# Extra storage for the keys and queries of the first attention, fp32 turns of the rounded activations, and a new written order of all engines

## The chip, the cores and the metric

The kernel runs on one core of a Trainium2 chip. The metric is the device time of one execution in microseconds (us). The kernel before took 265.31, 265.40 and 266.64 us in three runs, median 265.4. Of one more execution a profile was recorded; that one took 264.35 us. The engines are TensorE (PE, with weight loads shown apart as PEld), VectorE (DVE), ScalarE (ACT), GpSimd (POOL) and SyncE (SP, which only issues DMAs).

## The reference, cut to what matters

Two batches (B = 2) of 512 tokens with 128 features pass four blocks, each added to the running x after a scale by a tanh gate:

```python
x = x + tanh(g_xattn[0]) * L0_xattn(ctx, layernorm(x))      # 8 heads of 64, 512 queries, 512+77 keys
x = x + tanh(g_ffn[0])   * L0_ffn(layernorm(x))             # 8-bit rounding, 128->512, conv, silu, 512->128
x = x + tanh(g_xattn[1]) * L1_xattn(layernorm(x), ctx, ctx) # 16 heads of 8, 77 keys, rotary positions
x = x + tanh(g_ffn[1])   * L1_ffn(layernorm(x))             # 8 experts, top 2, and a shared one

# first attention, per batch and head
q = ln @ Wq; k, v = split(concat(layernorm(x), ln) @ Wkv)
attn = softmax((q / scale) @ k.T - max); out = (attn @ v) @ Wout

# rounding of the activations in the first feed-forward block
scale = 127.0 / clip(max(abs(h), -1), 1e-5)
hq = clip(round(h * scale), -128, 127) / scale              # h has 512 features per token
y = hq @ round_to_ternary(w2).T
```

## The kernel before, in words

The work is cut into items, each with a kind: x0 (turned, normalised input), q and k (queries and keys of one pair of heads; 4 pairs per batch), v (values), u (scores of one head for 128 queries; 64 of them), w (probabilities times values for one pair and 256 queries; 16), o (output projection), n (layer norm and rounding behind it), f1 to f4 (the feed-forward block: turn, product with w1 and convolution, rounding, product with w2), a1, a2, a3, a4, a6 (second attention: turn, queries, keys, scores, output), m1 to m4 (experts: turn, product up, router, product down). An item has stages: F and B are its first and second work on PE, A1 and A2 on ACT, D0 to D3 on DVE, P1 and P2 on POOL, Ca or Cd a copy out of PSUM by ACT or by DVE.

The order is written out by hand in one long string, PLAN. A word such as `f2:D1` puts the next item of that kind and stage at the end of that engine's list. `u:F6` also names the PSUM bank (0 to 7), and `a4:B+20@2` puts 20 turns of the identity matrix into bank 2 ahead of the stage; they compute nothing that is used. Each engine walks its list strictly in order, and semaphores carry the data dependencies. So an instruction that waits holds up everything behind it on its engine.

Three places are touched.

* Queries and keys. Pair g (0 to 7 over both batches) has its keys, split into an upper part KH and a rest KL, and its queries Q in one of two buffers, g mod 2. ACT writes the upper part (L863, L871), DVE the rest (L1033, L1040), and SP copies half of the keys across partitions. ACT waits before it writes until the last scores of pair g-2 are done.
* Rounding (f3, f4). ACT writes the rounded values plus a constant MAGIC as fp32 (L893). An own copy (L812 on ACT or L814 on DVE, four of each) takes MAGIC off and writes bf16 to QB. PE turns QB four 128x128 pieces at a time (L649) with a bf16 identity made by DVE. ACT copies the bf16 turns to QBT (L898), and PE multiplies by w2 (L731).
* Order. PLAN holds 85 identity turns in all (L518, `slot<-K`), most of them in the part behind the first attention.

The copies of turned probabilities of the second attention are L787 on ACT and L789 on DVE; its maximum is L1152 on DVE. The router is L1163 to L1230 on DVE.

Of the kernel before, what the change touches and what calls it, by code (L numbers as in the profile page):

```python
# [15 lines left out]
P = 128  # L16
# [109 lines left out]
a4:D1 f1:D1 f2:F6 a4:B a2:D1 f2:F7 a1:P1 a4:A1 f2:A1 a4:D1 a4:B a4:Ca f2:A1 a4:Ca f2:F3 f2:D1 f2:A1 f2:F6+4@2 f2:A2 f2:D1 f2:D2 f2:A1 a4:A1 a4:F0
f2:D1 a4:B+20@2 f2:A2 f2:A2 a4:D1 a4:F2 f2:D1 f2:D2 a4:D1 a4:A1 f2:D2 f2:A2 a4:B+11@7 a4:Ca a4:A1 f2:D2 f3:F6 f3:F7 f3:D1 a4:Ca f3:D1 f3:A1 f3:F4 a4:B
a4:F0 f3:Cd f3:F6 a4:D1 a4:Ca f4:F5 f3:A1 a6:F7 f4:A1 f3:D1 f3:D1 a4:A1 f3:Cd f4:B f3:A1 f3:A1 f4:F4 a4:F2 f4:A1 f3:Cd f4:D2 f3:Ca f4:F5 f4:B
f4:A1 f4:F6+2@6 f4:B a4:D1 f4:A1 f4:B+2@4 a4:A1 f4:D2 a4:B f4:P2 f4:D2 f4:D3 f4:D2 a4:F4 a4:Ca a1:F6 a4:D1 a4:B a1:A1 f4:P2 a4:A1 a2:F0 a4:Ca f4:D3
a1:P1 a1:F6+2@1 a2:D1 a4:B+9@1 a6:D1 a4:F2 a4:D1 a1:A1 a4:Ca a4:F0 a4:F4 a6:B a4:D1 a4:A1 a6:D2 a2:F6 a6:P2 a6:F7 a4:A1 a4:D1 a4:B a2:D1 a4:Ca a6:D3  # L130
a6:D1 a4:F2+8@6 a4:D1 a4:B a4:Cd a4:A1 a6:B a4:B a6:D2 m1:F6 a4:A1 a4:Ca a4:F0 a4:B a4:D1 a4:F4 a4:Cd a4:D1 a6:P2 a6:D3 m1:A1 a4:F6 a4:A1 m3:F2
a6:F3 m3:D1 a4:A1 a4:D1 m3:A1 a4:A1 a4:B a4:B a4:B a4:Ca m2:F0 a4:Ca m3:D2 m2:A1 a4:Ca a6:D1 a4:F4 m1:F2 m1:A1 a6:B m2:B a4:D1 m3:F2 m2:F6
a4:A1 m2:P1 m2:A2 a6:D2 a4:B m2:A1 m2:B a4:Ca m2:P1 a1:P1 m3:D1 m2:D1 m2:D2 m2:A2 m3:A1 m2:D1 a6:F3 m4:F0 m3:D2 m4:A1 m2:F4 m2:A1 a6:P2 a6:D1
m2:D2 m2:B m2:A2 m4:B a6:D3 m1:F6 a6:B m4:D2 m2:P1 m2:D1 m2:D2 m4:F0 m1:A1 m3:F2 m2:F6 a6:D2 a6:P2 m2:A1 m2:F4 m4:A1 m3:D1 m2:B m3:A1 m2:P1
m2:A2 m4:B m2:A1 m2:B+2@3 m3:D2 m4:D2 m2:P1 a6:D3 m4:F0 m2:D1 m2:A2 m2:D2 m2:D1 m2:F2 m4:A1 m2:D2 m2:B m2:A1 m1:F6 m2:A2 m1:A1 m4:B m2:P1 m2:D1
m4:F4 m4:A1 m4:D2 m3:F0 m2:F6 m2:D2 m4:B m4:F2 m2:A1 m3:D1 m3:A1 m3:D2 m4:D2 m2:B m4:A1 m2:F0 m2:A2 m4:F4 m2:B m2:A1 m4:B m2:P1 m2:D1 m4:A1
m2:A2 m2:D2 m4:F6 m2:P1 m2:D1 m2:D2 m4:D2 m4:B m4:A1 m4:F0 m4:A1 m4:B m4:B m4:D2 m4:D2 m4:D2
# [49 lines left out]
def mega_kernel(nc, x, ctx, ctxT, cols, wq, wk, wv, wout, w1T, w2T, l1w, bo, wgu, wdT, const, out):  # L187
    stack = ExitStack()
    with stack:
# [26 lines left out]
        identb = sb("identb", [P, P], BF16)  # L216
# [35 lines left out]
        KL = sb("KL", [P, 4, KEVEN], F32R)  # L252
        V = sb("V", [P, 5, IN0])
# [14 lines left out]
        QB = sb("QB", [P, 2, HID], BF16)  # L268
# [10 lines left out]
        PT1 = sb("PT1", [P, 2, 2 * KC1, N])  # L279
# [3 lines left out]
        HM = sb("HM", [P, QT, MT])  # L283
# [36 lines left out]
        identb_ready = sem("identb_ready")  # L320
# [16 lines left out]
        qb_copied = {"ACT": sem("qb_by_act"), "DVE": sem("qb_by_dve")}  # L337
# [466 lines left out]
        def copy_quantised(engine, by, item):  # L804
# [3 lines left out]
            if n > 2:  # L808
                engine.wait_ge(qbt_ready, n - 2)
# [549 lines left out]
```

## Time and profile before

| | |
|---|---|
| median of three runs | 265.4 us |
| profiled execution | 264.35 us |
| its span, first to last instruction | 262.4 us |
| PE busy | 254.0 us (97%) |
| DVE busy | 217.1 us (83%) |
| ACT busy | 192.2 us (73%) |
| POOL busy | 31.1 us (12%) |
| granted TensorE clock | full in all slices |

The span is shorter than the execution by 1.95 us, which lies around the program. Busy time of PE counts the identity turns as well, and a matmul's recorded length is longer than the distance to the next one: identity turns have a mean length of 0.276 us, and 18 of them in a row take 1.97 us from the first start to the next instruction's, 0.109 us each. So what PE really does is read from the distance between starts.

### The profile page before, as it was taken

The numbers are of one execution on the slowest core, as the hardware profiler recorded it, in microseconds if no ns is written. First come the engines' busy times: TensorE is split into PE (matmuls) and PEld (weight loads), VectorE is DVE, ScalarE is ACT, GpSimd is POOL, SyncE is SP. The second block draws the span as 40 slices with busy tenths as digits, with TensorE's granted clock in tenths as the row PEclk, the third lists the DMA queues.
The fourth block names the chain that finished last, engine by engine and source line by source line (L and its number), as shares of the span: only waits on it lengthen the run. The fifth ranks groups of instructions, "written<-read, shape, count | busy, mean of one in ns | idle before, by whom it ended". The sixth has DMA issues, their size and how long they took to land.

```text
span 262.4 us, 5607 instructions
## 1 busy us (share of the span) xinstructions
PE 254.0 (97%) x1869; PEld 189.2 (72%) x1869; DVE 217.1 (83%) x534; ACT 192.2 (73%) x463; POOL 31.1 (12%) x53
## 2 busy tenths in 40 slices
PE   7899999999999999999999999989999999999996
PEld 3568779779779878868787788767657565575675
DVE  5599979866766698998999787889899999899861
ACT  1689887788658678697899966179998699834551
POOL 3000002000000010201100102020003110424130
PEclk9999999999999999999999999999999999999999
DMA  6293491300400004300300000000000000000001
GB/s 184 56 239 97 95 343 32 90 4 0 95 1 1 2 0 101 86 0 4 92 4 0 0 2 0 4 0 1 2 0 4 4 1 0 2 9 4 21 10 40
DMA packets 8848, 10.70 MB, mean 41 GB/s; under 512 B 1115, under 2 KB 5877, under 8 KB 8821
## 3 DMA queue, kind: packets, MB, share of 16 engines
q1 hardware_dynamic: 7792, 9.70, 13.7%
q10 hardware_dynamic: 1029, 0.65, 0.8%
q8 instruction: 15, 0.25, 0.4%
q14 instruction: 12, 0.10, 0.1%
HBM read 4.99 MB, written 0.52 MB: 21 GB/s over the span
## 4 chain that ended last, share of the span: by engine, by line
PE 70%; DVE 18%; ACT 5%; issue 5%; POOL 1%; DVEq 0%; ACTq 0%; POOLq 0%
PE slot L518 19%; PE slot L608 13%; PE slot L589 6%; PE slot L590 6%; PE slot L564 3%; PE slot L615 3%; DVE mx L1152 3%; PE slot L570 2%; PE slot L761 2%; PE slot L755 2%; DVE RB L1157 2%; ACT S L910 2%; PE slot L706 2%; PE slot L749 2%; PE slot L579 2%
## 5 line engine op out<-in xcount | busy, mean ns | idle before, releaser
L1046 DVE TENSOR_REDUCE nm<-slot 128x1 f32<-128x589 f32 x64 | 47.6, 766 | 9.7 <-PE slot L590 9.3
L838 ACT ACTIVATE PR<-slot,nm 128x589 f32<-128x589 f32 x64 | 47.7, 749 | 9.3 <-DVE nm L1046 8.8
L518 PE MATMUL slot<-K,PR 128*128 128x128 f32 (+1 forms) x320 | 44.3, 276 | 0.2
L589 PE MATMUL slot<-KH,Q 128*128 128x296 f32 (+1 forms) x128 | 42.1, 345 | 0.2
L518 PEld LDWEIGHTS slot<-K,PR 128*128 128x128 f32 (+1 forms) x320 | 36.1, 142 | 8.1 <-ACT PR L838 5.0
L608 PE MATMUL slot<-PT,V 128*64 128x256 f32 (+1 forms) x320 | 38.1, 384 | 0.7 <-ACT PT L773 0.7
L773 ACT ACTIVATE PT<-slot 128x640 f32<-128x640 f32 x47 | 32.2, 705 | 8.3 <-PE slot L518 7.3
L590 PE MATMUL slot<-KL,Q 128*128 128x296 f32 (+1 forms) x128 | 36.1, 299 | 0.0
L910 ACT ACTIVATE S<-slot,mx 128x77 f32<-128x77 f32 x128 | 29.2, 365 | 6.3 <-DVE mx L1152 5.6
L608 PEld LDWEIGHTS slot<-PT,V 128*64 128x64 f32 (+1 forms) x320 | 22.1, 137 | 12.3 <-issue 3.5
L589 PEld LDWEIGHTS slot<-KH,Q 128*128 128x128 f32 x128 | 24.2, 189 | 3.6 <-issue 1.4
L590 PEld LDWEIGHTS slot<-KL,Q 128*128 128x128 f32 x128 | 24.3, 190 | 1.7 <-issue 1.4
L468 POOL TENSOR_TENSOR vex<-vex,mhalf 128x2 f32<-128x2 f32 (+1 forms) x15 | 10.8, 720 | 83.7 <-DVE vex L986 83.7
L484 POOL COPY REC<-rec 128x256 f32<-128x256 f32 x16 | 6.8, 422 | 111.4 <-DVE rec L1022 85.9
L775 DVE COPY PT<-slot 128x640 f32<-128x640 f32 x17 | 13.8, 815 | 1.8 <-PE slot L518 1.8
L1040 DVE TENSOR_TENSOR KL<-slot,KH 64x590 fp32r<-64x590 f32 x16 | 12.2, 765 | 2.7 <-ACT KH L871 2.3
L1152 DVE TENSOR_REDUCE mx<-slot 128x8 f32<-128x616 f32 x16 | 12.6, 794 | 0.3 <-PE slot L672 0.3
L838 ACT ACTIVATION_READ_ACCUMULATOR PR<-slot,nm 128x1 f32 x64 | 12.6, 197 | 0.0
L518 PE MATMUL slot<-K,S 128*128 128x128 f32 x80 | 11.7, 279 | 0.6 <-ACT S L910 0.6
L1033 DVE SCALAR_TENSOR_TENSOR Q<-slot,Q 64x512 fp32r<-64x512 f32 x16 | 11.0, 689 | 1.3 <-ACT Q L863 0.9
L871 ACT ACTIVATE KH<-slot 64x590 fp32r<-64x590 f32 x16 | 10.5, 654 | 2.3 <-PE slot L581 2.1
L518 PEld LDWEIGHTS slot<-K,S 128*128 128x128 f32 x80 | 8.8, 140 | 3.9 <-ACT S L910 3.5
(169 smaller groups left out, 478.2 us busy)
## 6 DMA issues: line engine op xcount, KB each, us to landing
KH<-KH SPq DMA_DIRECT2D x16, 147.5 KB, 2.5
KL<-KL SPq DMA_DIRECT2D x16, 147.5 KB, 2.6
CTT<-in_ctxT SPq DMA_DIRECT2D x1, 640.0 KB, 3.9
K<-in_const SPq DMA_DIRECT2D x1, 589.0 KB, 4.9
WGU<-in_wgu SPq DMA_DIRECT2D x1, 580.0 KB, 6.0
out<-X SPq DMA_DIRECT2D x8, 64.0 KB, 1.5
L1W<-in_l1w SPq DMA_DIRECT2D x1, 384.0 KB, 3.8
WD<-in_wdT SPq DMA_DIRECT2D x1, 320.0 KB, 6.5
```

The costliest lines, as they stand in the source:

```text
L518: return pe.transpose(dst, src, ident[0:p, 0:p])
L589: pe.matmul(W[:, K0 + lo:K0 + hi], q, KH[:, g % 4, lo:hi], start=True, stop=False)
L590: mm = pe.matmul(W[:, K0 + lo:K0 + hi], q, KL[:, g % 4, lo:hi], start=False, stop=True)
L608: mm = pe.matmul(W[e * DH0:(e + 1) * DH0, 0:N], V[0:r, c, h * DH0:(h + 1) * DH0], PT[0:r, s, c, e, :], start=(c == 0), stop=(c == 4))
L773: engine.activation(dst, src, ACT.Copy).then_inc(pt_copied["ACT"], 1)
L775: engine.tensor_copy(dst, src).then_inc(pt_copied["DVE"], 1)
L838: act.activation(PR[:, s, :], W[:, K0:K0 + KEYS0], ACT.Exp, bias=nm0[:, s:s + 1], accum_out=sum0[:, b, p * 2 + f, t, e:e + 1]).then_inc(pr ...
L910: act.activation(S1[:, s, j * C:(j + 1) * C], W[:, at:at + C], ACT.Exp, bias=mx1[:, s, j:j + 1]).then_inc(exp1_ready, 1)
L1033: dve.scalar_tensor_tensor(out=Q[o, s, e, :], in0=W[r, 0:S], scalar=float(DH0) ** 0.5, in1=Q[r, s, e, :].bitcast(F32), op0=ALU.mult, op1=A ...
L1040: dve.tensor_tensor(KL[r, s, :], W[r, K0:K0 + KEVEN], KH[r, s, :].bitcast(F32), ALU.subtract).then_inc(k_ready, 1)
L1046: dve.tensor_reduce(nm0[:, s:s + 1], W[:, K0:K0 + KEYS0], AX.X, ALU.max, negate=True).then_inc(max_ready, 1)
L1152: dve.tensor_reduce(mx, w, AX.X, ALU.max, negate=True).then_inc(max1_ready, 1)
```

## The change

* A table HOME gives each of the eight pairs its place: pairs 0 to 3 and 6, 7 alternate between the two old buffers, pair 4 has a third place and pair 5 a fourth. The two new ones lie in memory of PT1 and HM, which the second attention and the experts fill later; before the first writes there, the engines now wait for the last scores of pair 5 (`guests_gone`). A pair waits only for the former user of its own place (`home_left`), so pairs 4, 5, 6 and 7 wait for no, no, pair 2 and pair 3.
* The copy to QB, its bf16 identity and its semaphores are gone. PE turns the fp32 values with the MAGIC constant still in them, into a whole bank, and the ACT copy to QBT takes MAGIC off. The third rounding now waits until the first one has been turned on PE, before until it had been copied.
* PLAN is new from end to end, with 31 identity turns in place of 85, and 47 copies of u on ACT and 17 on DVE as before; of the 16 copies of a4 15 are on ACT and 1 on DVE, before 14 and 2.

```diff
+HOME = (0, 1, 0, 1, 2, 3, 0, 1)
+GUEST = 8 * (1 + max(g for g, home in enumerate(HOME) if home > 1))
@@ PLAN, two of its lines
-w:F4 n:P2 a2:F2+5@0 w:A1 a1:F3 n:D3 w:D1 a1:A1 a2:D1 o:F1 o:F0 a4:F2 o:D1 o:D1 a4:F0 n:P2 a2:F7 a1:P1 a4:D1 n:D3 a4:A1 f1:F6+18@5 f1:A1 a4:F4
+a4:F2+7@0 w:D1 a4:D1 o:F0+2@1 o:F4 f4:D3 a1:F5 o:D1 a4:A1 a4:F6 o:D1 a4:D1 a1:A1 a4:B a2:F4 a4:F0 n:P2 a4:A1 n:D3 a1:P1 f1:F5 a4:D1 a4:Ca a4:F2
+        KHG, KLG = [GUESTS[:, i * 4 * KEVEN:(i + 1) * 4 * KEVEN].rearrange("p (k c) -> p k c", k=4) for i in range(2)]
+        QG = QGUEST[:, 0:4 * S].rearrange("p (g e q) -> p g e q", g=2, e=2)
-        QB = sb("QB", [P, 2, HID], BF16)
+        def keys(own, guest, head):
+            home = HOME[head // 2]
+            return (own, guest)[home // 2][:, home % 2 * 2 + head % 2, :]
+        def home_left(engine, g):
+            before = [k for k in range(g) if HOME[k] == HOME[g]]
+            if before:
+                engine.wait_ge(front_done, NTH[KINDS["u"][8 * before[-1] + 7]] + 1)
+        def guests_gone(engine):
+            engine.wait_ge(front_done, NTH[KINDS["u"][GUEST - 1]] + 1)
@@ f4, PE
-                    pe.wait_ge(*quantised(n))
-                    pe.wait_ge(identb_ready, 1)
-                    Wb = W[:, 0:256].bitcast(BF16)
+                    pe.wait_ge(rounded, n)
                     for c in range(HC):
-                        mm = pe.transpose(Wb[:, c * P:(c + 1) * P], QB[:, (n - 1) % 2, c * P:(c + 1) * P], identb[:])
+                        mm = turn(W[:, c * P:(c + 1) * P], QM[(n - 1) % 2][:, c * P:(c + 1) * P])
@@ q and k, ACT
-                    if g >= 2:
-                        act.wait_ge(front_done, NTH[KINDS["u"][8 * (g - 1) - 1]] + 1)
+                    home_left(act, g)
@@ f3 and f4, ACT
-                        act.wait_ge(*quantised(n - 2))
+                        act.wait_ge(front_done, NTH[KINDS["f4"][n - 3]] + 1)
-                    act.activation(QBT[:, (n - 1) % 2, :], W[:, 0:256].bitcast(BF16), ACT.Copy).then_inc(qbt_ready, 1)
+                    act.activation(QBT[:, (n - 1) % 2, :], W[:, 0:HID], ACT.Copy, bias=-MAGIC).then_inc(qbt_ready, 1)
```

What the new order does is seen in the rows of three places. The first is DVE in batch 1, at the rounding of the feed-forward block, in the kernel before: aq2 is a tile's scale, QB the copy, mx1 a maximum of the second attention, X the result of f4.

```order
L1105 TENSOR_REDUCE aq2<-slot3 128x1
L1106 TENSOR_SCALAR aq2<-aq2 128x1
L1107 RECIPROCAL aq2<-aq2 128x1
L1108 TENSOR_SCALAR aq2<-aq2,g2 128x1
L814 TENSOR_SCALAR QB<-W2 128x512
L814 TENSOR_SCALAR QB<-W1 128x512
L1202 SCALAR_TENSOR_TENSOR X<-slot2,aq2,X1 128x128
L975 BN_STATS bnx<-X 128x6
L976 BN_AGGR mvx<-bnx 128x2
L1152 TENSOR_REDUCE mx1<-slot1 128x8
```

The same place on DVE in the changed kernel, where its lines are numbered a few higher:

```order
L1111 TENSOR_REDUCE aq2<-slot3 128x1
L1112 TENSOR_SCALAR aq2<-aq2 128x1
L1113 RECIPROCAL aq2<-aq2 128x1
L1114 TENSOR_SCALAR aq2<-aq2,g2 128x1
L1208 SCALAR_TENSOR_TENSOR X<-slot3,aq2,X1 128x128
L981 BN_STATS bnx<-X 128x6
L982 BN_AGGR mvx<-bnx 128x2
L1158 TENSOR_REDUCE mx1<-slot1 128x8
```

The copies are gone from between the last scale and the first result; a third one of batch 1 stood a little earlier. The second place is DVE at its last layer norm (the last XN of the kernel), before; lg, hot and cwt belong to the router of the first half of batch 1.

```order
L1167 MAX_INDEX idx<-top,lg 128x8 x2
L1169 TENSOR_TENSOR lg<-lg,top 128x16
L1212 TENSOR_TENSOR hot<-K,idx 128x32
L1214 TENSOR_TENSOR hot<-hot 128x2x8
L1220 SCALAR_TENSOR_TENSOR HM<-SHT,slot1 128x2x64
L1222 SCALAR_TENSOR_TENSOR HM<-HM,slot1 128x2x64
L1226 TENSOR_REDUCE rt<-lg 128x2
L1227 RECIPROCAL rt<-rt 128x2
L1228 SCALAR_TENSOR_TENSOR cwt<-lg,hot 128x16
L1230 TENSOR_TENSOR cwt<-cwt,rt 128x16
L1251 SCALAR_TENSOR_TENSOR X<-slot0,tg,X1 128x128
L989 TENSOR_SCALAR XN<-X1,mvx,vex 128x128 x2
```

And now:

```order
L1182 SCALAR_TENSOR_TENSOR HM<-slot1,HM 128x512
L1255 TENSOR_TENSOR HM<-HM,slot1 128x512
L995 TENSOR_SCALAR XN<-X1,mvx,vex 128x128 x2
L1169 COPY lg<-slot0 128x16
L1172 MAX top<-lg 128x8 x2
L1173 MAX_INDEX idx<-top,lg 128x8 x2
L1175 TENSOR_TENSOR lg<-lg,top 128x16
L1182 SCALAR_TENSOR_TENSOR HM<-slot3,HM 128x512
```

The router of that half, and the result of one more tile, have moved behind the last norm. The third place is PE at the last turn of the experts' input (`K,XN`), before; L706 and L749 are the two products of a tile of 512 columns, L755 and L756 the product down.

```order
L706 MATMUL slot1<-WGU,LT 128x512
L749 MATMUL slot1<-WGU,LT 128x512
L518 MATMUL slot3<-K,XN 128x128 x2
L755 MATMUL slot0<-WD,CTT 128x128 x4
L756 MATMUL slot0<-WD,CTT 128x128
L518 MATMUL slot2<-K,HM 128x128 x4
L518 MATMUL slot2<-K,HM 64x128
L699 MATMUL slot0<-WGU,LT 128x136 x2
```

And now:

```order
L536 MATMUL slot0<-K,XN 128x128 x2
L771 MATMUL slot1<-WD,CTT 128x128 x4
L772 MATMUL slot1<-WD,CTT 128x128
L536 MATMUL slot0<-K 128x128
L536 MATMUL slot3<-K,HM 128x128 x4
L536 MATMUL slot3<-K,HM 64x128
L722 MATMUL slot2<-WGU,LT 128x512
L765 MATMUL slot2<-WGU,LT 128x512
L722 MATMUL slot1<-WGU,LT 128x512
```

The four products of the first two tiles of batch 1, which stood ahead of this turn, stand behind it (the fourth a little further down), with two single identity turns among them.

## Rows read from the trace of the kernel before

**Rows 1.** The page: busy time per engine and granted clock in 40 slices.

```profile
PE 254.0 (97%) x1869; PEld 189.2 (72%) x1869; DVE 217.1 (83%) x534; ACT 192.2 (73%) x463; POOL 31.1 (12%) x53
...
PEclk9999999999999999999999999999999999999999
```

**Rows 2.** Busy time in stretches: PE, PEld, DVE, ACT, POOL, clock, DMA.

```profile
8.00:162.00 154.00, 152.82 (x1122) 121.20 (x1123) 127.49 (x276) 123.40 (x251) 11.83 (x23) 1.00 0.21 57
...
174.70:241.80 67.10, 64.38 (x538) 42.32 (x536) 62.42 (x169) 53.99 (x176) 10.56 (x14) 1.00 0.01 3
241.80:262.40 20.60, 18.12 (x108) 13.41 (x108) 12.08 (x35) 9.12 (x22) 3.83 (x4) 1.00 0.08 23
```

**Rows 3.** Waits in 8:162: who, for whom, us in total, times, longest.

```profile
PEld slot L518 <- ACT PR L838: 5.0, 17, 0.4
```

**Rows 4.** What ended the idle time ahead of L871 (keys) and L863 (queries).

```profile
  PE slot L581: 2.1, 3
...
  PE slot L570: 1.7, 1
```

**Rows 5.** PE in order of time: start, length, instructions.

```profile
136.45 0.60 PE L518 MATMUL slot<-K,YC 128*128 128x128 f32 x4
...
142.10 0.40 PE L649 MATMUL slot<-identb,QB 128*128 128x128 bf16 x4
...
171.55 2.13 PE L518 MATMUL slot<-K 128*128 128x128 f32 x18
173.52 0.52 PE L518 MATMUL slot<-K,XN 128*128 128x128 f32 x2
```

**Rows 6.** Waits of DVE in 166:241, first and last of six.

```profile
DVE RC L1142 <- PE slot L664: 0.7, 1, 0.7
...
DVE mx L1152 <- PE slot L672: 0.3, 1, 0.3
```

**Rows 7.** Groups of instructions: xcount, busy us, mean ns, idle before.

```profile
L898 ACT ACTIVATE QBT<-slot 128x512 bf16<-128x512 bf16 x8 | 4.7, 593 | 0.3 <-PE slot L649 0.2
...
L814 DVE TENSOR_SCALAR QB<-W 128x512 bf16<-128x512 f32 x4 | 1.7, 427 | 0.2
...
L789 DVE COPY PT<-slot 128x640 f32<-128x640 f32 x2 | 1.6, 818 | 0.0
```

**Rows 8.** DVE in order of time.

```profile
174.76 0.69 DVE L1091 TENSOR_TENSOR XL<-slot,XH 128x512 fp32r<-128x512 f32 x1 [0.40 <-PE slot L672]
...
190.19 0.79 DVE L1152 TENSOR_REDUCE mx<-slot 128x8 f32<-128x616 f32 x1
190.90 0.68 DVE L1105 TENSOR_REDUCE aq<-slot 128x1 f32<-128x512 f32 x1
...
241.81 1.04 DVE L989 TENSOR_SCALAR XN<-X,mvx,vex 128x128 f32<-128x128 f32 x2
...
247.30 0.17 DVE L1163 COPY lg<-slot 128x16 f32<-128x16 f32 x1 [0.23 <-PE slot L699]
...
249.01 0.29 DVE L1220 SCALAR_TENSOR_TENSOR HM<-SHT,slot 128x128 f32<-128x128 f32 x1 [0.34 <-ACT SHT L918]
...
250.60 0.35 DVE L1251 SCALAR_TENSOR_TENSOR X<-slot,tg,X 128x128 f32<-128x128 f32 x1 [0.16 <-DVE cwt L1230]
```

**Rows 9.** PE in order of time, last stretch.

```profile
242.55 1.02 PE L706 MATMUL slot<-WGU,LT 128*128 128x512 f32 x2
...
244.27 0.39 PE L518 MATMUL slot<-K,XN 128*128 128x128 f32 x2
...
249.96 1.02 PE L749 MATMUL slot<-WGU,LT 128*128 128x512 f32 x2
250.82 1.02 PE L706 MATMUL slot<-WGU,LT 128*128 128x512 f32 x2
...
259.58 0.49 PE L756 MATMUL slot<-WD,CTT 64*128 64x128 f32 x2
```

**Rows 10.** Line L761: lengths min/median/max, first and last start.

```profile
L761 PE MATMUL slot<-TH x10: 592/592/1219, 1.5 to 6.8; 128*128 128x512 f32 x10
```

More of the change, by code:

```diff
@@ L426, in double @@
                     r, o = slice(e * DH0, (e + 1) * DH0), slice((1 - e) * DH0, (2 - e) * DH0)
-                    s = (2 * g + e) % 4
-                    for part, signal in ((KH, k_upper), (KL, k_ready)):
+                    for own, guest, signal in ((KH, KHG, k_upper), (KL, KLG, k_ready)):
                         sp.wait_ge(signal, 2 * g + e + 1)
-                        sp.dma_start(part[o, s, :].bitcast(F32), part[r, s, :].bitcast(F32)).then_inc(k_doubled[g % 2][e], 16)
+                        part = keys(own, guest, 2 * g + e).bitcast(F32)
+                        sp.dma_start(part[o], part[r]).then_inc(k_doubled[g % 2][e], 16)
             double(0)
@@ L802, in copy_values @@
                 engine.tensor_copy(dst, slot(item)[0:rows, 0:n * 512]).then_inc(v_copied["DVE"], 1)
-        def copy_quantised(engine, by, item):
-            n = upto(item)
-            engine.wait_ge(rounded, n)
-            if n > 2:
-                engine.wait_ge(qbt_ready, n - 2)
-            dst, src = QB[:, (n - 1) % 2, :], QM[(n - 1) % 2]
-            if by == "ACT":
-                engine.activation(dst, src, ACT.Copy, bias=-MAGIC).then_inc(qb_copied["ACT"], 1)
-            else:
-                engine.tensor_scalar(dst, src, MAGIC, None, ALU.subtract).then_inc(qb_copied["DVE"], 1)
         @block.scalar
@@ L866, in first @@
                     g = b * NP0 + item[2]
-                    if g >= 2:
-                        act.wait_ge(front_done, NTH[KINDS["u"][8 * (g - 1) - 1]] + 1)
+                    home_left(act, g)
                     for e in range(2):
                         r = slice(e * DH0, (e + 1) * DH0)
-                        act.activation(KH[r, (2 * g + e) % 4, :], W[r, K0:K0 + KEVEN], ACT.Copy).then_inc(k_upper, 1)
+                        act.activation(keys(KH, KHG, 2 * g + e)[r], W[r, K0:K0 + KEVEN], ACT.Copy).then_inc(k_upper, 1)
                 elif kind == "f1":
@@ L1031, in first @@
                         r, o = slice(e * DH0, (e + 1) * DH0), slice((1 - e) * DH0, (2 - e) * DH0)
-                        s = (n - 1) % 2
-                        dve.scalar_tensor_tensor(out=Q[o, s, e, :], in0=W[r, 0:S], scalar=float(DH0) ** 0.5,
-                                                 in1=Q[r, s, e, :].bitcast(F32), op0=ALU.mult,
+                        q = queries(n - 1, e)
+                        dve.scalar_tensor_tensor(out=q[o], in0=W[r, 0:S], scalar=float(DH0) ** 0.5,
+                                                 in1=q[r].bitcast(F32), op0=ALU.mult,
                                                  op1=ALU.subtract).then_inc(q_ready, 1)
```

112 lines of the change are left out of this document (57 added, 55 removed).

## The prediction, made before the changed kernel was run

> **What bounds the kernel now.** I read the page first. PE is busy for 254.0 of 262.4 us, at the full granted clock in all 40 slices [rows 1]. That looks like a kernel bound by PE from end to end, so the second view is the busy time by stretches [rows 2]. Up to 162 us PE works on scores, turns and products without a break (152.8 of 154.0 us), while DVE and ACT have 27 and 31 us to spare. From 174.7 to 241.8 us PE is also shown as busy (64.4 of 67.1), but there it is not the bound: 76 of its instructions are turns of the identity matrix, put where it would otherwise wait. DVE is busy for 62.4 us there, and its waits from 166 to 241 us are six and sum to 2.6 us [rows 6]; the rest of its idle time is the short distance between small instructions. So this stretch, from the split of batch 1's rounded input at 174.76 us to the last layer norm at 241.81 us [rows 8], lasts as long as DVE's list. Behind it PE leads again: its last turn of the experts' input starts at 244.27, the last product down at 259.58 us [rows 9].
>
> So the sum goes along three pieces: PE up to about 175 us, DVE from 175 to 242, PE from there. Of the new order I price what crosses the borders of these pieces.
>
> **The homes.** The trace shows idle time of ACT ahead of the writes of keys and queries only for their own projections (2.1 us in three waits, 1.7 in one) and never for scores, which is what a taken buffer would look like [rows 4]. The wait that the new homes remove costs nothing now. They allow the projections of pair 5 to stand 8 to 10 us of work earlier, ahead of the dense part; the same instructions run. I put them at 0. Their direct worth is bounded by the waits for the exponentials that they could help to spread, 5.0 us in 17 waits of the weight loads up to 162 us [rows 3], of which most lies beside running matmuls. The waits for the guests' last user stand ahead of writes that come after all 64 scores in every list, so they are met: 0. SP copies the same halves.
>
> **Piece one, PE.** A rounded tile is now turned in fp32. Four such turns are recorded at 0.60 us together, four bf16 ones at 0.40 [rows 5], so +0.20 a tile and, for the four tiles of batch 0, +0.8. For the four of batch 1 the place is in DVE's piece, where PE has its 76 fillers to give up: 0 (0.8 if that cover is gone). Ahead of batch 1's f1 stand 9 identity turns instead of 7, at 1.97 / 18 = 0.109 us each [rows 5]: +0.2. The 18 within f1 go, but they stood before a layer norm of DVE that PE has to wait for anyway. So +1.0.
>
> At this place the Trainium skill has two rules. "FP8 and Floating Point Precision", in TensorE Precision Notes, gives true fp32 four passes through the array; "TensorE: Matmul & The Clock Gate", in Terms, says that the transpose mode makes fp32 four times as fast. By the first alone each tile would cost three times its bf16 turns on top, by both together nothing. The rows of this case lie between the two, and the sum uses the rows.
>
> **Piece two, DVE.** Between its two marks the new list has nothing that was not there, and lacks these:
> - one maximum of the second attention, which moves ahead of the first mark: 190.19 to 190.90, 0.71 [rows 8];
> - one copy of turned probabilities, given to ACT: 0.82 [rows 7];
> - the three QB copies of batch 1: 3 x 0.427 = 1.28 [rows 7];
> - both halves of the router for the first half of batch 1, moved behind the last norm: the other half's router runs from 247.30 to 250.60, less its two waits of 0.34 and 0.16: 2.8 [rows 8];
> - one result of an expert tile, moved behind as well: 0.35 [rows 8].
>
> Together 6.0 us. The maximum that moves ahead of the first mark falls into the end of piece one, where DVE has some room; I charge nothing for it, and it is in the range with 0.7. ACT gains a copy and loses one of batch 1's four to QB, and with 54.0 of 67.1 us [rows 2] it isn't next. Its read of the turns is now fp32 rather than bf16: 0.593 us for 128x512 [rows 7], which I keep. The path from a rounded tile to its turn loses the copy, 0.43 us on DVE. The third rounding now waits for PE's turn of the first instead of its copy; that turn stands ahead of it in the work anyway, since ACT's own copy of the first turn comes before the third rounding in its list.
>
> What is late next is PE. It has to do 54 identity turns less (85 to 31), some 5.9 us, and 3.4 us of products leave the piece, so it has more room than DVE. So the last norm starts at 241.81 + 1.0 - 6.0 = 236.8.
>
> **Piece three, PE.** Before, PE came to the last turn of the experts' input only at 244.27, since two products of a tile stood ahead of it (from 242.55 [rows 9]). Now that turn starts when the norms are there, about 0.6 behind 236.8, at 237.4. Behind it PE did 244.27 to 259.99 (the last product down starts at 259.58 and has 0.41 to run), 15.7 us. Added are four products of 512 columns, each 250.82 - 249.96 = 0.86 [rows 9], 3.4 us, and two identity turns, 0.2. That ends at 256.7, against 260.0: -3.3. But DVE now has 12.1 + 3.2 = 15.3 us of work in this stretch of some 20 [rows 2], and each tile is a chain from PE over ACT, POOL and DVE back to PE, twice; I allow 0.9 us of waits, two and a half of the 0.34 us that the router had [rows 8]. The end moves by -2.4.
>
> **Sum.** +1.0 - 6.0 and in piece three +2.6 against the mark (3.6 of work and 0.9 of waits, less 1.9 that PE was late before): -2.4 us. The profiled execution would go from 264.35 to 261.95 us. The median of the runs is 265.4, 1.05 above that execution, so I state 265.4 - 2.4 = 263.0 us. About 0.5% (1.3 us) is what can be told from no change.
>
> **Rivals.**
> 1. *The last stretch takes it back.* If each of the four expert tiles of batch 1 waits for its router and its chain on all its links, at 0.8 us (the 0.34 and 0.16 of the router and 0.3 of PE's own hand-over), that is 3.2 us instead of 0.9, and the order ahead of 162 us gives nothing: 265.3 us. For it: DVE and PE are both dense there now. Against it: PE has its choice of four products in a row while it waits.
> 2. *PE's total decides.* 54 identity turns less, 5.9 us, eight fp32 tiles more, 1.6: -4.3, and 261.1 us. That holds if the waits that the fillers covered are gone and not only uncovered. For it: fewer fillers stand also in the stretch where ACT and DVE lost work. Against it: DVE's list has no such waits to lose [rows 6].
> 3. *Slower: the clock.* The fillers kept PE's recorded share high from 175 to 242 us. With 54 less, and some 12 us of real waits there, the granted clock could fall from 2.4 to 1.2 GHz between the turns of batch 1's rounding. The program's first matmuls show both lengths: 1.219 us at most, 0.592 in the median for 512 columns [rows 10]. Ten us at the low level hold about 8 us of PE work, which would take 8 more, of which the 2 to 4 us of room there are free: +5 on the forecast, 268 us. It decides from the point at which PE rests for longer than any wait of today. Against it: 31 fillers stay, and PE's real work fills four fifths of that stretch. The skill speaks on both sides of this one: the page "TensorE: Matmul & The Clock Gate" warns of idle gaps between bursts (in Why this matters for your kernels), and in Part 4 says that transposes don't count as busy for the gate; by the latter the removed turns did nothing for the clock. The trace can't tell them apart, since the clock is full throughout.
> 4. *Slower: crowding ahead of 162 us.* All 64 score tiles have new neighbours. If each waits 0.08 us more for its exponential, PE, which has no room there, is 5 us later: 268 us. The row for these waits (5.0 in 17) says that a shift either way of 2 us is easy and one of 5 is not.
> 5. *The homes do more than I say*, by letting the first piece close up: it is within the lower end, at -2 on the forecast.
>
> **How the numbers follow.** Forecast 0.50 (its own range 261.8 to 264.4, a tenth of it above 264.07); rival 1 0.20; rival 2 with 5 0.17; rivals 3 and 4 together 0.13. Faster by over 0.5%: 0.45 + 0.17 = 0.62. Within: 0.05 + 0.20 = 0.25. Slower: 0.13. The range goes from 260.4 (rival 2 with part of 5) to 266.5 (rival 1 with the 0.7 and 0.8 left out above, below 268) and leaves out some 0.15.
>
> **What would show it.** DVE between its first mark and the last norm: 61 us instead of 67.05, with waits still under 3 us. The last turn of the experts' input within 1 us of the norm, at 237 to 238 us; from there to the end of PE 19 to 20.5 us. Four fp32 turns of a rounded tile at 0.6 us. The clock full. The score stage ending within 1 us of where it does now. Wrong would be: DVE's waits in its piece over 4 us; a first piece that is over 2 us shorter or longer, for which I have no row; or a low clock.

## The result

The changed kernel takes 267.73 us (median of 8 runs, 266.85 to 268.63), the kernel before 265.4 us on the same chip (median of 8, 264.64 to 266.64): 1.009 times as long, interval 1.0069 to 1.0111. So it is slower by 2.3 us, where 2.4 us less was forecast, and outside the range that was given. The profiled execution took 268.4 us, its span is 266.6. Its mean granted clock is 0.981, as in three of the eight runs; in the other five it is 0.987.

The page of the kernel after, busy time and granted clock, to be held against [rows 1]:

```profile
PE 254.3 (95%) x1815; PEld 188.3 (71%) x1815; DVE 214.6 (80%) x528; ACT 191.0 (72%) x460; POOL 30.8 (12%) x53
...
PEclk9999999999999999999999999989689999999999
```

PE has 54 instructions less and is busy for longer, and one slice has a 6 where before all were full. That is the first hint. The busy time in the prediction's three pieces, cut at the first turn of normalised input, at the split of batch 1's rounded input and at the last layer norm (columns: stretch, length, PE, PEld, DVE, ACT, POOL, clock, DMA):

```profile
8.67:177.96 169.29, 166.50 (x1210) 129.84 (x1209) 138.40 (x309) 128.57 (x271) 13.12 (x26) 1.00 0.19 52
177.96:242.53 64.57, 58.88 (x470) 39.42 (x471) 56.47 (x148) 49.68 (x160) 9.88 (x13) 0.92 0.01 3
242.53:266.60 24.07, 21.73 (x129) 16.00 (x127) 14.73 (x52) 11.24 (x29) 5.21 (x5) 1.00 0.07 20
```

DVE's list in the middle piece is 56.47 us; the nearest row of before has 62.42 in almost the same piece [rows 2]. That is the 6.0 us that the prediction took out. But the piece went only from 67.05 to 64.57 us, and in it the clock is 0.92. Where it is low, cut close:

```profile
177.80:181.20 3.40, 3.37 (x11) 1.97 (x9) 2.83 (x6) 2.89 (x11) 1.28 (x2) 0.51 0.00 0
188.10:194.90 6.80, 6.68 (x30) 5.46 (x29) 4.40 (x12) 3.68 (x11) 0.00 (x0) 0.50 0.01 2
```

Half of full is the lower level, 1.2 GHz. PE in order of time around the second stretch, with its waits in brackets (L536 is every turn, L688 the score products of the second attention, S its exponentials, YC the output of the convolution; `slot<-K` alone is an identity turn):

```profile
184.01 0.79 PE L688 MATMUL slot<-KBD,Q 32*128 32x308 f32 x4 [0.74 <-DVE YC L1105]
187.15 0.77 PE L536 MATMUL slot<-K,S 128*128 128x128 f32 x5 [2.35 <-ACT S L914]
187.84 1.21 PE L688 MATMUL slot<-KBD,Q 32*128 32x308 f32 x4
188.98 1.50 PE L536 MATMUL slot<-K,YC 128*128 128x128 f32 x4
190.27 2.13 PE L536 MATMUL slot<-K 128*128 128x128 f32 x9
192.19 1.70 PE L536 MATMUL slot<-K,YC 128*128 128x128 f32 x7
```

PE stands for 2.35 us until the exponentials of the second attention are there, then works, and its clock falls 0.95 us after it began again. In before, 35 identity turns stand at this place, among the stages of the convolution and of the second attention:

```profile
178.32 0.60 PE L518 MATMUL slot<-K 128*128 128x128 f32 x4
180.28 2.40 PE L518 MATMUL slot<-K 128*128 128x128 f32 x20
183.97 1.42 PE L518 MATMUL slot<-K 128*128 128x128 f32 x11
```

The new PLAN has none there before the nine at 190.27. By pieces, before has 25, 60 and 0 identity turns in its trace, after 9, 20 and 2.

Within the low stretch four turns of YC take 1.50 us, where four take 0.60 at full clock [rows 5]. Nine identity turns, made to fill a wait, now take 1.92 us from start to start and stand in the way. DVE in the same place, kept waiting by PE:

```profile
190.52 0.69 DVE L1111 TENSOR_REDUCE aq<-slot 128x1 f32<-128x512 f32 x1 [0.57 <-PE slot L536]
...
193.37 0.69 DVE L1111 TENSOR_REDUCE aq<-slot 128x1 f32<-128x512 f32 x1 [1.66 <-PE slot L536]
...
199.15 0.35 DVE L1208 SCALAR_TENSOR_TENSOR X<-slot,aq,X 128x128 f32<-128x128 f32 x1 [1.45 <-PE slot L747]
```

These three are 3.7 us of DVE's waits. In the whole piece DVE is idle for 64.57 - 56.47 = 8.1 us, before for 67.05 - 62.43 = 4.6.

The last piece is the same at any clock seen: 24.07 us against 20.60 [rows 2]. PE at its last turn of the experts' input and at the end:

```profile
242.47 0.63 PE L715 MATMUL slot<-WGU,LT 128*128 128x136 f32 x4
242.93 0.71 PE L536 MATMUL slot<-K,HM 128*128 128x128 f32 x5
243.47 1.06 PE L771 MATMUL slot<-WD,CTT 128*128 128x128 f32 x8
244.46 0.48 PE L772 MATMUL slot<-WD,CTT 64*128 64x128 f32 x2
244.88 0.44 PE L536 MATMUL slot<-K,XN 128*128 128x128 f32 x2
...
263.77 0.48 PE L772 MATMUL slot<-WD,CTT 64*128 64x128 f32 x2
```

The norm starts at 242.53, its turn at 244.88, 2.35 us later. PE isn't waiting; it is late, as it was before (2.46 us, [rows 8, 9]).

One more thing has to be taken off before two executions are compared. The opening matmuls (five products of zeros, recorded as ten), which read no input, took this long in before and in after:

```profile
1.45 5.96 PE L761 MATMUL slot<-TH 128*128 128x512 f32 x10 [1.45 <-DVE TH L992]
```

```profile
1.45 7.38 PE L777 MATMUL slot<-TH 128*128 128x512 f32 x10 [1.45 <-DVE TH L998]
```

More of them are long in the second execution: the median length is 1.06 us, before 0.59. That looks like a low clock that lasted longer, but the granted clock reads full there in both traces, so the cause isn't shown. The change doesn't touch this code: in the profiles of the twelve experiments below the first turn of normalised input starts anywhere between 7.3 and 8.8 us (before 7.25, after 8.67). So below, pieces are counted from that turn, and 1.4 of the 4.2 us between the two spans are no part of the change.

### The profile page after: what moved, and what is told of

It is laid out like the page before. It is cut to its first block, busy times and chain, and to the rows that moved or that the text cites. A ratio compares the mean times of both kernels' runs of the same rounds, so it can differ in the third digit from the quotient of the medians.

```text
span 266.6 us, 5494 instructions
## 1 busy us (share of the span) xinstructions
PE 254.3 (95%) x1815; PEld 188.3 (71%) x1815; DVE 214.6 (80%) x528; ACT 191.0 (72%) x460; POOL 30.8 (12%) x53
## 4 chain that ended last, share of the span: by engine, by line
PE 76%; DVE 12%; ACT 6%; issue 5%; POOL 0%; DVEq 0%; ACTq 0%
PE slot L536 24%; PE slot L626 13%; PE slot L607 6%; PE slot L608 6%; PE slot L582 3%; PE slot L777 3%; PE slot L771 3%; ACT S L914 3%; PE slot L633 2%; PE slot L588 2%; DVE YC L1103 2%; PE slot L688 2%; PE slot L722 2%; PE slot L765 2%; PE slot L597 2%
## 5 line engine op out<-in xcount | busy, mean ns | idle before, releaser
L536 PE MATMUL slot<-K,PR 128*128 128x128 f32 (+1 forms) x320 | 44.8, 277 | 0.5 <-ACT PR L844 0.3
L536 PEld LDWEIGHTS slot<-K,PR 128*128 128x128 f32 (+1 forms) x320 | 36.2, 142 | 12.0 <-ACT PR L844 8.0
L789 ACT ACTIVATE PT<-slot 128x640 f32<-128x640 f32 x47 | 32.7, 704 | 9.1 <-PE slot L536 8.8
L607 PE MATMUL slot<-KH,Q 128*128 128x296 f32 x96 | 29.9, 330 | 0.0
L608 PE MATMUL slot<-KL,Q 128*128 128x296 f32 x96 | 27.0, 300 | 0.0
L607 PEld LDWEIGHTS slot<-KH,Q 128*128 128x128 f32 x96 | 18.2, 189 | 1.9 <-DVE PT L791 0.6
L608 PEld LDWEIGHTS slot<-KL,Q 128*128 128x128 f32 x96 | 18.2, 190 | 0.2
L536 PE MATMUL slot<-K,S 128*128 128x128 f32 x80 | 12.6, 295 | 3.0 <-ACT S L914 2.9
L536 PEld LDWEIGHTS slot<-K,S 128*128 128x128 f32 x80 | 9.8, 151 | 6.5 <-ACT S L914 5.6
L805 ACT ACTIVATE PT<-slot 128x640 f32<-128x640 f32 x15 | 10.8, 739 | 3.8 <-PE slot L536 3.7
L688 PE MATMUL slot<-KBD,Q 32*128 32x308 f32 x64 | 11.7, 483 | 1.3 <-DVE YC L1105 0.7
L862 ACT ACTIVATE RB<-slot 128x256 f32<-128x256 f32 x16 | 6.1, 383 | 8.2 <-PE slot L626 7.9
```

The lines of the kernel that those rows point to most:

```text
L536: return pe.transpose(dst, src, ident[0:p, 0:p])
L607: pe.matmul(W[:, K0 + lo:K0 + hi], q, keys(KH, KHG, g)[:, lo:hi], start=True, stop=False)
L608: mm = pe.matmul(W[:, K0 + lo:K0 + hi], q, keys(KL, KLG, g)[:, lo:hi], start=False, stop=True)
L688: mm = pe.matmul(W[:, n * 512:n * 512 + G1 * C], Q1[rows, t * P:(t + 1) * P], KBD[rows, b], start=True, stop=True)
L789: engine.activation(dst, src, ACT.Copy).then_inc(pt_copied["ACT"], 1)
```

## The experiments

They ran in four groups, each beside the kernel before on the same chip: e1 to e4, e5 to e8, e9 to e11, and e12. The median of before was 265.29, 265.56, 265.15 and 265.08 us there, and the ratio is to that; so across groups ratios and pieces are compared, not medians. A median is of 12 runs, for e3, e4, e8 and e12 of 5 or 6. The table gives the pieces of each profiled execution, from the starts of the three instructions named above: one, first turn of normalised input to the split; two, to the last norm; three, to the end.

| kernel | median us | ratio to before (95%) | one | two | three | sum | clock |
|---|---|---|---|---|---|---|---|
| before | 265.4 | | 167.51 | 67.05 | 20.60 | 255.16 | 1.000 |
| after | 267.73 | 1.0090 (1.0069 to 1.0111) | 169.29 | 64.57 | 24.07 | 257.93 | 0.981 |
| e1 | 265.27 | 0.9995 (0.9982 to 1.0009) | 169.29 | 62.19 | 24.06 | 255.54 | 1.000 |
| e2 | 266.18 | 1.0034 (1.0018 to 1.0049) | 170.13 | 61.99 | 24.07 | 256.19 | 1.000 |
| e3 | 269.92 | 1.0163 (1.0141 to 1.0186) | 170.58 | 66.36 | 24.07 | 261.01 | 0.973 |
| e4 | 267.66 | 1.0093 (1.0072 to 1.0115) | 169.57 | 67.82 | 20.60 | 257.99 | 1.000 |
| e5 | 266.41 | 1.0031 (1.0011 to 1.0050) | 167.95 | 67.50 | 20.62 | 256.07 | 1.000 |
| e6 | 266.27 | 1.0025 (1.0005 to 1.0045) | 166.94 | 69.06 | 20.61 | 256.61 | 0.974 |
| e7 | 265.40 | 1.0000 (0.9985 to 1.0016) | 169.28 | 61.98 | 24.07 | 255.33 | 1.000 |
| e8 | 268.38 | 1.0092 (1.0065 to 1.0120) | 169.70 | 64.39 | 24.07 | 258.16 | 0.987 |
| e9 | 264.95 | 1.0006 (0.9988 to 1.0025) | 169.30 | 62.19 | 24.08 | 255.57 | 1.000 |
| e10 | 265.64 | 1.0024 (1.0005 to 1.0042) | 169.27 | 62.19 | 24.09 | 255.55 | 1.000 |
| e11 | 265.39 | 1.0012 (0.9995 to 1.0030) | 167.96 | 67.24 | 20.62 | 255.81 | 1.000 |
| e12 | 268.26 | 1.0130 (1.0096 to 1.0165) | 170.61 | 63.49 | 24.07 | 258.18 | 0.998 |

**e1, e2: the new kernel with its waits filled.** 35 identity turns more: 9 (in e2, 18) in the bank of batch 1's f1 itself, 6 and 20 ahead of the stages at which PE waited.

```diff
-... f2:D1 a4:F4 f2:A1 ... f2:D2 a4:B f2:A2
+... f2:D1 a4:F4+6@5 f2:A1 ... f2:D2 a4:B+20@0 f2:A2
@@ f1, batch 1, PE
+OWN = {("f1", 1): 9}                        # 18 in e2
+                            for _ in range(OWN.get(item, 0)):
+                                turn(W[:, 3 * P:4 * P], ident)
```

> The changed kernel with 35 more identity turns where its trace shows PE waiting: 9 within batch 1's f1, 6 ahead of the scores of tile 2 of the second attention, 20 ahead of the turns of tile 1's second half. Nothing else is changed. Theory A (the low clock costs the time): no low stretch or one short one, and the median falls from 267.7 to 263 to 265 us. Theory B (the new order is longer by its own waits, the clock only follows from them): the clock is full and the time stays within 1 us of 267.7. Theory C (the fp32 turns or the homes cost it): the same as B.

> As the run before, but with 18 identity turns within f1 rather than 9, as many as the kernel before had there. Theory A: the first low stretch, at 178 us, goes for sure; if 9 were too few, this one is faster by 1 to 2 us, else slower by at most the 1 us that nine turns take. Theory B: within 1 us of the changed kernel or slower.

In e1 the clock is full, piece two is 2.4 us shorter and nothing else differs: 265.27 us, just over theory A's range and far from B's and C's. So the low clock is real and costs 2.4 us. The 9 in f1 cost nothing (piece one as in after), the 9 more of e2 cost 0.8 of piece one, against 9 x 0.109 = 1.0 worked out: the wait there holds the first nine and not the second. But e1 only draws level with before. The forecast of a gain fails at full clock too.

**e3: the new order and homes, with the bf16 copies and turns of before.**

```diff
-                    pe.wait_ge(rounded, n)
+                    pe.wait_ge(*quantised(n))
...
-PLAN: f3:A1
+PLAN: f3:A1 f3:Ca          # Ca for four, Cd for four
```

> The changed kernel's order and homes, but the rounding as before: the copies to QB are back (each right behind its rounding's place in the order, three of batch 1's on DVE as before), with bf16 turns. Theory A and B: slower than the changed kernel by what the copies cost on DVE in its piece, 1 to 2 us, so 268.5 to 270 us. Theory C for the fp32 turns: faster, 266 us or less.

2.2 us over after and within what A and B expect, with two low stretches in the profiled execution (mean clock 0.973, in the four other runs 0.987). It leaves open how much of that is the copies and how much the clock; e12 settles it.

**e4: the old order, with the homes and the fp32 turns.** PLAN of before without its copies of f3.

> The order of before without the eight copies to QB, with the new homes and the fp32 turns. Theory A and B: faster than before by the 1.3 us of DVE's three copies in its piece less up to 0.8 us of fp32 turns in batch 0: 264.4 to 265.4 us, clock full, since the 85 identity turns stand. Theory C: 1 to 3 us slower than before, 266.5 to 268.5 us.

2.3 us slower at a full clock, in theory C's range: piece one is 2.1 longer, piece two 0.8, although DVE's list in it is 1.1 shorter (61.37 against 62.43). Up to the w stage at 140 us nothing is lost, then 1.9 us within ten. ACT in order of time in e4:

```profile
139.02 1.20 ACT L868 ACTIVATE Q<-slot 64x512 fp32r<-64x512 f32 x2
143.12 0.78 ACT L897 ACTIVATE W<-slot,COL,aq 128x512 f32<-128x512 f32 x1 [2.91 <-PE slot L536]
143.80 0.74 ACT L844 ACTIVATE PR<-slot,nm 128x589 f32<-128x589 f32 x1
```

L897 is the third rounding. Its tile is free only when PE has turned the first value, and PE, in its own order, first has 20 products of a w stage:

```profile
140.04 2.38 PE L626 MATMUL slot<-PT,V 128*64 128x256 f32 x20
142.35 0.66 PE L536 MATMUL slot<-K,W 128*128 128x128 f32 x4
144.00 0.38 PE L607 MATMUL slot<-KH,Q 128*128 128x296 f32 x1 [1.00 <-issue]
```

The exponentials of the first attention stand behind L897 in ACT's list. The prediction had named this new wait and called it met.

**e5: e4 with a third tile for rounded values.**

```diff
-        QM = W1[:], W2[:].rearrange("p c d -> p (c d)")
+        QM = W1[:], W2[:].rearrange("p c d -> p (c d)"), sb("Q3", [P, HID])[:]
@@ f3, ACT; f4 on PE reads the same tile
-                    if n > 2:
-                        act.wait_ge(front_done, NTH[KINDS["f4"][n - 3]] + 1)
-                    act.activation(QM[(n - 1) % 2], W[:, 0:HID], ACT.Identity, bias=COL[:, NCOL - 1:NCOL],
+                    if n > 3:
+                        act.wait_ge(front_done, NTH[KINDS["f4"][n - 4]] + 1)
+                    act.activation(QM[(n - 1) % 3], W[:, 0:HID], ACT.Identity, bias=COL[:, NCOL - 1:NCOL],
```

> The old order with the new homes and the fp32 turns, as in the run before it that came to 267.66 us at a full clock, but with a third tile for the rounded values, so that the third rounding waits for the turn of nothing: ScalarE stood for 2.9 us ahead of that rounding (140.2 to 143.1 us). Theory C (the wait of the third rounding holds ScalarE's list, and the exponentials queued behind it hold TensorE): 265.3 to 266.0 us, 1.7 to 2.3 less. Rival (the fp32 turns and homes cost this themselves: 8 x 0.2 = 1.6 us of turns): 267.0 or more.

At the same place ACT goes through (the third tile is shown as Q):

```profile
140.02 1.19 ACT L868 ACTIVATE Q<-slot 64x512 fp32r<-64x512 f32 x2
141.24 0.78 ACT L897 ACTIVATE Q<-slot,COL,aq 128x512 f32<-128x512 f32 x1
```

1.25 us by the medians, 1.6 by the ratios and 1.6 in piece one: the wait was the cause. The median, 266.41, lies between the 265.3 to 266.0 expected and the rival's 267.0; e11 looks at the rest.

**e6: the kernel before without its identity turns.** All 85 taken out of PLAN, such as `f1:F6+18@5` to `f1:F6`.

> The kernel before with its 85 identity turns left out and nothing else changed. Theory A (the identity turns hold the clock; without them it falls between the steps of batch 1's rounding): granted clock under 0.985 on average, with a stretch at 1.2 GHz between 166 and 245 us, and 267.5 to 271 us. Rival (the identity turns fill waits and do nothing for the clock, as turns through the array would do by the rule of the Trainium skill's page TensorE: Matmul & The Clock Gate, Part 4): clock full and 264.5 to 265.5 us, equal or somewhat faster.

The clock falls, in two stretches that begin in the same part of the kernel:

```profile
173.60:180.40 6.80, 6.43 (x22) 4.62 (x23) 5.52 (x11) 4.78 (x13) 1.41 (x2) 0.50 0.00 0
183.80:190.60 6.80, 5.89 (x23) 4.23 (x24) 5.93 (x10) 6.80 (x25) 0.00 (x0) 0.50 0.00 0
```

Each begins within a long wait of PE, the first just before its end:

```profile
173.78 0.69 PE L518 MATMUL slot<-K,XN 128*128 128x128 f32 x2 [1.80 <-DVE XN L1275]
184.58 1.32 PE L518 MATMUL slot<-K,S 128*128 128x128 f32 x5 [2.59 <-ACT S L910]
```

So in the kernel before, too, the identity turns hold the clock. The time was expected at 267.5 to 271 and is 266.27: piece two is 2.0 us longer and piece one 0.6 shorter, where 25 identity turns are gone. That they stood on PE's path is the likely reason; it wasn't tested. Theory A's mechanism holds, its price was set too high.

**e7, e8: which of e1's identity turns are needed.** e7 has the 26 in PLAN alone, e8 none of these and 14 in batch 1's f1.

> The new kernel with the 26 identity turns at the two later places alone (6 and 20), without the 9 in batch 1's f1. If the clock needs the fill only where it fell (from 177 us on): full clock and 264.5 to 265.3 us, up to 1.0 us (9 x 0.109) under the run with all 35. If the first low stretch is set by the wait at 166 us ahead of it: the first low stretch stays (mean 0.987 or less) and 266.5 to 267.5 us.

> The new kernel with 14 identity turns within batch 1's f1 and none at the two later places. If the wait at 166 us starts the fall: the first low stretch goes, the second (188 us) stays: mean clock 0.985 to 0.99 and 266.5 to 267.5 us. If the later waits (176.7, 184.0, 187.2) do it alone: both low stretches stay, and 267.7 to 269 us.

e7 is e1 again (265.40, 0.1 over its range; all 12 runs have a mean clock of 0.994 or more). PE there, in place of the 2.35 us wait:

```profile
181.35 0.82 PE L536 MATMUL slot<-K 128*128 128x128 f32 x6
182.40 0.79 PE L688 MATMUL slot<-KBD,Q 32*128 32x308 f32 x4 [0.23 <-DVE YC L1105]
183.67 2.40 PE L536 MATMUL slot<-K 128*128 128x128 f32 x20 [0.49 <-ACT PT L805]
185.91 0.71 PE L536 MATMUL slot<-K,S 128*128 128x128 f32 x5
```

The profiled execution of e8 has the second low stretch and not the first:

```profile
188.40:195.20 6.80, 6.23 (x29) 5.62 (x28) 4.40 (x12) 3.33 (x11) 0.00 (x0) 0.50 0.00 0
```

Its time is over what was expected: piece two is 64.39, nearly after's 64.57. So the second stretch costs nearly all, and the first some 0.2 us. The traces of after and e7 agree: counted from the split, the turn of S comes at 9.19 us in after (187.15 - 177.96) and at 9.09 in e7 (185.91 - 176.82). The first stretch ends at 181.2, and from 180 to 188 us PE is busy for 4.6 of 8 us only and had time to make good.

That e8's 14 turns removed the first stretch doesn't follow. It begins 0.16 us ahead of the split, and e7's first extra turns stand 4.5 us behind the split. Up to there PE does the same in after and e7, at the same distances to within 0.02 us as far as the clock is full in both, and yet only after's profiled execution has the stretch. So executions of the same instructions differ there. By their mean clocks five of after's own eight runs have only as much low clock as the second stretch gives (0.987; with both it is 0.981).

**e9: e7 with the third tile of e5.**

> The new kernel with the 26 identity turns at the two later places and the third tile for the rounded values. In the old order the third tile was worth 1.25 us. Theory D (the new order already puts the turn early enough, so that little is left of that wait): within 0.4 us of the 265.4 us of the run with the 26 alone. Rival (the wait of the third rounding is also why the first piece of the new order is 1.8 us over that of before): 264.0 to 264.6 us, and the split of batch 1's rounded input 168.0 to 168.5 us behind the first turn of normalised input instead of 169.3.

264.95 us; the ratio, 1.0006, is 0.2 us over e7's. Piece one is 169.30, as without, and not the rival's 168.0 to 168.5. Theory D holds: the new order doesn't pay that wait.

**e10: the 20 at one place alone.**

> The new kernel with the 20 identity turns at one place alone, ahead of the turn at 187 us that waited 2.3 us. If the clock falls for what stands just ahead of a low stretch: the 6.8 us at 188 us go and at most the 3.4 us at 178 us stay in some runs: 265.0 to 265.8 us. If the rest needs fill as well: a mean clock of 0.987 or less and over 266.5 us.

265.64 us, as expected; the profiled execution is at full clock. The 20 do the work: none of the 36 runs of e7, e9 and e10 has a mean clock under 0.994, and none of the 14 of after and e8 has one over 0.987.

What is left is 3.4 us of low clock (a mean of 0.994) in some runs: four of 12 in e10, one in e7, two in e9, none of the 24 of e1 and e2, which also have turns in f1, ahead of the place of the first stretch. No such run was profiled, so where it lies is open, and so is whether the 6 do anything. Its price is open too: these seven runs have spans of 264.6 to 264.9, the others of e7, e9 and e10 262.7 to 264.1. That is more than the 0.2 us above, but the spans hold the opening, which differs by up to 1.5 us.

**e11: e5 without guests** (without the third and fourth place for keys and queries). HOME = (0, 1, 0, 1, 0, 1, 0, 1).

> The old order with fp32 turns and the third tile for rounded values, but each pair's keys and queries in the two own homes (no guests). Theory (homes cost and bring nothing): 266.4 us as with the guests, within 0.4. What then stands against the kernel before (+0.85 us) is the 0.8 of the fp32 turns of batch 0. Rival (the guests cost something, as by keys and queries that lie apart): 265.5 to 265.9 us.

265.39 us, with pieces within 0.26 us of e5's. That is under both ranges; by the ratios e11 is 0.5 us faster than e5, and the intervals overlap. Homes bring nothing in the old order; whether they cost some tenths isn't settled.

e11 is also the kernel before with the fp32 turns and a third tile, and nothing else. It shows what the removed copies are worth in the old order. Piece two, from split to norm:

```profile
175.66:242.90 67.24, 64.66 (x536) 42.96 (x536) 61.33 (x166) 53.41 (x175) 10.50 (x14) 1.00 0.01 3
```

DVE's list is 1.1 us shorter than before's 62.43, and the piece is 0.2 us longer. At the first result of the feed-forward block in batch 1 DVE now waits for PE:

```profile
193.68 0.20 DVE L1113 TENSOR_SCALAR aq<-aq,g 128x1 f32<-128x1 f32 x1
194.84 0.35 DVE L1207 SCALAR_TENSOR_TENSOR X<-slot,aq,X 128x128 f32<-128x128 f32 x1 [0.96 <-PE slot L746]
```

At this place before has two of the copies, 0.91 us from 193.33 on. PE works from 191.60 to 194.33 on products of the second attention (48 records) and comes to L746 behind them. So here the copies filled time in which DVE would have waited for PE.

**e12: e3 with e7's 26 identity turns.**

> The new order and homes with the bf16 copies and turns of the rounded values put back, and the 26 identity turns at the two later places, which held the clock full in the fp32 version (265.4 us; 255.3 us from the first turn of normalised input to the end). It gives the price of the copies in the new order at a full clock. From the prediction's rows: batch 0's four tiles 0.8 us faster on TensorE, batch 1's three copies on VectorE 3 x 0.43 = 1.3 us slower: 0.5 us over the fp32 version, 265.9 us. Rival (the copies also stand in the lists of ScalarE and VectorE ahead of work that TensorE waits for, as the low-clock pair of runs says, 269.9 against 267.7): 2 us or more over it, 267.4 to 268 us.

268.26 us, 2.9 over e7 (3.4 by the ratios): 1.3 in piece one, 1.5 in piece two. The rival was right, and its 267.4 to 268 still somewhat low. DVE's list in piece two, e7 and then e12, is 1.35 us longer, the three copies [rows 7]:

```profile
176.82:238.80 61.98, 57.46 (x496) 38.82 (x497) 56.45 (x147) 49.53 (x160) 9.90 (x13) 1.00 0.01 3
```

```profile
178.56:242.05 63.49, 56.75 (x496) 38.11 (x497) 57.80 (x150) 50.23 (x161) 9.86 (x13) 1.00 0.01 3
```

In batch 0, where the prediction had charged the fp32 turns 0.8 us, leaving them out made piece one longer in this order: there, too, a copy costs more than the longer turn. The copies were put right behind their roundings; another place for them was not tried.

No version here is faster than the kernel before; e1, e7, e9 and e11 equal it within their intervals.

## Why the prediction was wrong

It forecast 263.0; the kernel takes 267.7. The largest step that failed is the clock, taken as full with 54 identity turns less. Two more failed at full clock: that piece two shrinks as much as DVE's list, and that PE starts its last turn of the experts' input as soon as the norms are there. And piece one was put 0.8 us too short, for a reason that is in part open. The 4.7 us are, by steps (e7, the new kernel at a full clock, stands for the pieces):

| step | predicted | measured | off by |
|---|---|---|---|
| piece one | +1.0 | +1.8 | 0.8 |
| piece two, DVE's list | -6.0 | -6.0 | 0 |
| piece two, as long as that list | -6.0 | -5.1 | 0.9 |
| piece three against the mark | +2.6 | +3.5 | 0.9 |
| clock full | 0 | +2.3 (267.73 - 265.40) | 2.3 |

The four that are off sum to 4.9. They come from profiled executions and medians mixed, so 0.2 is left.

*The clock.* The step that failed is the choice of rival 3 as a side case. Its place was right (between the turns of batch 1's rounding), and so was its cause (identity turns taken away); e1, e7, e10 and e6 show it from both sides. The count was off: the prediction has 76 identity turns in this piece of before and 54 less after, and the traces have 60 and 20. Its price of 5 was twice too high: it took 10 us of PE work at half speed to be on the path. After has 10.2 us of low clock, yet 3.4 of them lie where PE had slack. Against it I had set that PE's real work fills four fifths of the piece, a mean. What counted was one place, the 2.35 us wait that 20 identity turns fill in e10. Shorter waits stand ahead of it (0.78, 0.35 and 0.74 us, from 175.9 us on); whether they matter was not tested. The prediction also weighed the Trainium skill there. "TensorE: Matmul & The Clock Gate", in Part 4, has it that turns in transpose mode don't count as busy for the gate: by that rule after would have kept before's clock, and e7 after's. The runs disagree: with 26 such turns and nothing else the mean clock is 0.994 or more in all 12 runs of e7, without them 0.981 or 0.987 in all eight of after. The warning of idle gaps on the same page (Why this matters for your kernels) agrees with the runs in kind: it is the filling of the 2.35 us wait that holds the clock.

*Piece two.* The list of edits on DVE was right to 0.1 us. That the piece lasts as long as the list was not: DVE's idle time there rises from 4.6 to 5.5 us even at full clock (61.98 - 56.45). The waits named in e7 are short ones for PE, 0.8, 0.7 and 0.6 us at a reciprocal of the second attention, the scales and a result. The old order shows it most clearly: a list 1.1 us shorter gave a piece 0.2 us longer (e11), where the prediction priced the same copies at 1.28 us. In the new order they are worth 1.5 (e12). So DVE wasn't the only bound of this piece even before: at the first results of the feed-forward block PE comes close behind it.

*Piece three.* PE's work was sized right: from its last turn of the experts' input to its end 19.3 us (244.88 to about 264.2) against 15.7 + 3.6 = 19.3. The 0.9 us of waits that were added on top did not lengthen the piece. The step that failed is "that turn starts when the norms are there", worth 1.9. Moving the four 512-wide products behind the turn left a product down of two tiles, the turns of HM and the router product ahead of it, and PE arrived as late as before. With 1.75 too little and 0.9 too much, 0.9 remain.

*Piece one.* The fp32 turns are charged 0.8. In the old order, once the wait of the third rounding is removed, piece one is 0.45 longer (e11), and in the new order the bf16 version is the slower one (e12). What was missing is the order: its waits for the exponentials of the first attention are, for after,

```profile
PEld slot L536 <- ACT PR L844: 8.0, 20, 0.9
```

against 5.0 in 17 [rows 3], and 5.0 in 17 in e11 as well. That is rival 4's crowding at a fraction of its price. It is read from the trace and was not tested by itself; some 1.3 us of piece one are put down to it by what is left, and that stays open.

*The third rounding.* "That turn stands ahead of it in the work anyway" is true of the new order (e9) and false of the old (e4, 1.6 us of piece one). The statement was made of the change and held; the reason for it, ACT's list, was not enough, since what matters is PE's place for the turn.

*The homes.* Worth 0, as said, in the old order, to within some tenths. What they allow the new order to do was not tried by itself.

## What to carry to other kernels

Ahead of taking filler work out of a kernel whose clock is full throughout, look for the longest wait that it covers, not for the mean load: take out the filler of that place alone first, and read the granted clock around it. When a buffer's release moves from one engine to another, look for what stands in front of the new releaser in its own list, and for what is queued behind the waiting instruction. A list that is cut by 6 us on the leading engine gave 5.1 here, and a cut of 1.1 us gave nothing in the old order (e11); and the next engine in line had its own lateness at the border, which has to be read from its list ahead of the mark and not from what lies behind it.

## What was not expected of the hardware

* A low clock costs by what stands in it. 6.8 us at half clock were worth 2.2 to 2.4 us (piece two: e8 64.39, e1 62.19, e7 61.98), 3.4 us where PE had slack 0.1 to 0.2 in the one trace that has them.
* It comes and goes between executions of the same code: three of after's eight runs have a mean clock of 0.981 and five 0.987.
* In after it fell while PE was at work again, 0.95 us after the end of its wait, and lasted longer than the wait had. In e6 both stretches began before PE's wait was over.
* The opening differs between executions of the same code: the first turn of normalised input starts anywhere from 7.25 to 8.8 us. Medians of kernels move by some tenths with the share of late ones, so differences below 0.5 us were read from pieces.
* Four turns of fp32 take 0.60 us where four of bf16 take 0.40 [rows 5], yet in the new order the whole version with bf16 turns is 2.9 us slower (e12), for its copies. In the old order it is the faster one by 0.65 us from the first turn on (before against e11).
